# Layer-norm statistics stored in one transfer and read with a stride, and the second and third batch prepared in another order, in a gated cross-attention and expert kernel

## The chip, the cores and the metric

The kernel runs on one core of a Trainium2 chip. The metric is the device time of one launch in microseconds (us), lower is better. One core has TensorE (PE, matrix products), VectorE (DVE), ScalarE (ACT), GpSimd (POOL) and SyncE (SP), which here issues nearly all plain transfers. Each engine works through its own instructions in the order in which they are written, and waits on semaphores for the others.

## What is computed

```python
x = x + jnp.tanh(g_xattn[0]) * _L0_xattn_ref(ctx_1024, _layernorm(x, axis=-1), ...)
x = x + jnp.tanh(g_ffn[0]) * _L0_ffn_ref(_layernorm(x, axis=-1), ...)

def _L0_xattn_ref(x, latents, ...):            # x: the context, latents: the normalised x
    xn, ln = _layernorm(x, gamma_media, beta_media), _layernorm(latents, gamma_lat, beta_lat)
    q = ln @ Wq + bq
    kv = jnp.concatenate([xn, ln], axis=1) @ Wkv + bkv
    k, v = jnp.split(kv, 2, axis=-1)           # 8 heads of 128
    attn = jax.nn.softmax(einsum('bhid,bhjd->bhij', q * DH ** -0.5, k))
    return (attn @ v) @ Wo + bo
```

There are 16 batches of 256 rows of x and 256 rows of context, 256 wide. The attention has 8 heads of 128 over 512 keys (256 of the context, 256 of the latents). The second half, `_L0_ffn_ref`, sends each of the 4096 rows to 2 of 8 experts (256 to 1024 to 256). Everything is float32; each product is made of three products of a high and a low part.

## The kernel before

**Attention by steps.** A step `i` (0 to 127) is one head `h = i % 8` of one batch `b = i // 8`. In step `i` TensorE makes, in this order: the scores of step `i`; the transposes of the probabilities of step `i-1` (`turn`); the units `k` and `q` of step `i+1`, one unit `v`, and the unit `o` of step `i-1` (weights times values); and the output projection of step `i-2`. The units take turns in a ring of three PSUM banks, so the unit `o` of a step starts when the `k` unit of that step has been read. ACT rounds each unit to its high part (`kt_hi`, `qt_hi`, ...), DVE subtracts it for the low part (`kt_lo`, `qt_lo`, ...). DVE also takes the maxima of the scores (`smax`, then `nbias`), ACT the exponentials, and POOL multiplies by the reciprocal sums (`probs`).

**The operand of a batch.** All keys, values and queries of a batch are products with one operand, `kvt`: the normalised rows of x and context, transposed. For batch 0 it is made on the spot. For each later batch `c` it is made ahead, from transposed copies of x and context that the host supplies:

- `load(c)` brings the plain rows (`x_raw`, `c_raw`); `load_turned(c)` brings the transposed ones into `zin` (named `z_turned` in the trace). SP issues both.
- DVE takes mean and variance of the plain rows (`prepare_a(c, 0)` for x, `prepare_a(c, 1)` for the context; BATCH_NORM rows in the trace). POOL turns them into a negated mean and a factor for each row, in `norms` (`prepare(c)`).
- `spread_norms(c)` on SP writes `norms` to DRAM and reads it back to all 128 partitions, as the tile `spread`, so that each column of `zin` finds its mean and its factor.
- DVE adds the mean (`centre(c, k)`) and multiplies by the factor (`normalise_turned(c, k)`), for k = 0 and 1. ACT applies gamma and beta (`scale_turned(c)`, L1047), and POOL splits the result into the high and low part of `kvt` (`split_kv(c)`, L912 and L914).

For batch 1 the calls stand in steps 3 to 5: `centre` and `normalise_turned` in 3 and 4, `scale_turned` at the end of step 4, `split_kv` in step 5 after `probs`. The first unit that needs the `kvt` of batch 1 is the `v` unit of step 5. For batches 2 and later they stand at steps h = 6, 7, 0, 1 and 3. DVE's `prepare_a(2, 0)` stands at the end of step 2.

**Weights.** Each weight is loaded raw, ACT makes the high part (`hi_weights`), DVE or POOL the low part (`lo_weights`). The pieces are `q0`, `k0` (heads 0 and 1), `v0`, `k1`, `q1` (the other six heads), `v1`, `o0`, `o1`. The raw pieces `k1`, `q1`, `o0`, `o1` lie where `spread` lies later, so SP waits for `k1` to be split before it fills `spread`.

**SP's own order.** SP is one queue of issues. Its waits hold up what is written behind them, as here, where the rows of batch 2 stand behind two waits of `spread_norms(1)`:

```python
            load_turned(1)
            spread_norms(1)
            sp.wait_ge(s_routing, N_ROUTING)
            ...
            load(2)
            load_turned(2)
            spread_norms(2)
```

After the attention, the expert part runs over 40 tiles of rows. The change does not touch it.

Of the kernel before, what the change touches and what calls it, by code (L numbers as in the profile page):

```python
# [190 lines left out]
def build(nc, A):  # L191
# [10 lines left out]
    with ExitStack() as top:  # L202
# [45 lines left out]
        with ExitStack() as third:  # L248
# [33 lines left out]
            spread=nc.dram_tensor("mean_and_factor", (B, 2, KEYS), F32, kind="Internal").ap(),  # L282
# [56 lines left out]
def layer(nc, programs, A, sem, alloc, space, early, step, work, lists, ident, iota8, lane, dram,  # L339
# [6 lines left out]
    with ExitStack() as ctx:  # L346
# [141 lines left out]
        s_win = {name: sem(name + "_in") for name in ("k0", "k1", "q0", "q1", "v0", "v1", "o0", "o1")}  # L488
# [166 lines left out]
        def columns(name, at, width, by):  # L655
# [8 lines left out]
                  columns("q1", FIRST_W, rest, "dve"), columns("v1", HALF, HALF, "pool")]  # L664
        for c in range(2):
            heads = slice(c * H // 2, (c + 1) * H // 2)
            pieces.append(("o" + str(c), A["L0_xattn_Wo"][c * INNER // 2:(c + 1) * INNER // 2, :]
                           .rearrange("(h p) n -> p h n", p=P), raw["o" + str(c)], [w[:, heads, :] for w in wo], "dve"))
# [22 lines left out]
        def _(sp):  # L691
# [16 lines left out]
            def load_turned(c):  # L708
# [5 lines left out]
                for name, cols in (("x_turned", slice(T, KEYS)), ("ctx_turned", slice(0, T))):  # L714
                    sp.dma_start(zin[:, :, cols], A[name][c].rearrange("(k p) t -> p k t", p=P)).then_inc(s_turned_in, 16)

            def spread_norms(c):
# [13 lines left out]
                sp.dma_start(spread[:, :, :].rearrange("p r t -> p (r t)"),  # L731
                             dram["spread"][c].rearrange("r t -> (r t)").partition_broadcast(P)).then_inc(s_spread, 16)
# [4 lines left out]
            load_weights("o0", "o1")  # L737
# [8 lines left out]
            load_turned(1)  # L746
            spread_norms(1)
# [4 lines left out]
            load(2)  # L752
# [70 lines left out]
        def _(pool):  # L823
# [22 lines left out]
            def prepare(c):  # L846
# [5 lines left out]
                if c >= 2:  # L852
                    pool.wait_ge(s_norms_out, 64 * (c - 1))
# [102 lines left out]
            for i in range(STEPS + 2):  # L956
# [7 lines left out]
                if i == 5:  # L964
# [44 lines left out]
        def _(act):  # L1009
# [30 lines left out]
            def scale_turned(c):  # L1040
# [3 lines left out]
                for k in range(KD):  # L1044
                    for s in range(2):
                        cols = slice(s * T, (s + 1) * T)
                        last = act.activation(zt[:, k, cols], zin[:, k, cols], ACT.Identity,  # L1047
# [78 lines left out]
            for i in range(STEPS + 2):  # L1126
# [23 lines left out]
                if i == 4:  # L1150
# [52 lines left out]
        def _(pe):  # L1203
            def unit(kind, at):
# [4 lines left out]
                if kind in "kq":  # L1209
                    b, h = at // H, at % H  # L1210
                    if at in (0, FIRST_HEADS):
                        weights_split(pe, kind + str(int(at > 0)))
                    if (kind, at) == ("q", 0):
# [68 lines left out]
            def out_proj(n):  # L1282

                b, h = n // H, n % H
                if n == 0:
                    weights_split(pe, "o0")
                    weights_split(pe, "o1")
# [164 lines left out]
        def _(dve):  # L1452
# [365 lines left out]
            def centre(c, k):  # L1818
# [3 lines left out]
                own.mark(dve.tensor_tensor(zin[:, k, :], zin[:, k, :], spread[:, 0, :], ALU.add))  # L1822

            def normalise_turned(c, k):
                own.wait()
                dve.tensor_tensor(zin[:, k, :], zin[:, k, :], spread[:, 1, :], ALU.mult).then_inc(s_zin, 1)

            for i in range(STEPS + 2):
# [12 lines left out]
                for u in steps[i]:  # L1841
# [16 lines left out]
                if i in (3, 4):  # L1858
                    normalise_turned(1, i - 3)
# [7 lines left out]
                if i == 1:  # L1867
                    lo_weights(dve, "dve", "o0", "o1")
# [101 lines left out]
```

## Time and profile before

| | before |
|---|---|
| median of 3 runs | 1546.45 us (1545.08 to 1552.04) |
| the profiled execution | 1541.18 us, of which the span is 1539.5 us |
| TensorE busy | 1491.3 us, 97% of the span |
| DVE, ACT, POOL busy | 1140.1, 954.1, 568.9 us |
| granted TensorE clock over the span | 0.994 of full speed |

The profiled execution is 5.3 us shorter than the median of the runs. The span runs from its first to its last instruction. All rows are of that execution, with times counted from the span's start.

### The profile page before, as it was taken

The page shows a single profiled execution, that of the slowest core. Times are in us where ns is not written, and L with a number is a line of the kernel's source. Part 1 is how long each engine was busy: PE and PEld are TensorE (multiplying, and loading weights), DVE is VectorE, ACT ScalarE, POOL GpSimd, SP SyncE. Part 2 cuts the span into 40 slices and gives each one's busy share as a digit, 9 for nine tenths or more (in the row PEclk, how much of TensorE's full clock was granted, in tenths as well). Part 3 has the DMA queues.
Part 4 walks back from the last instruction along what each step waited for, and adds up shares of the span by engine and source line. Part 5 has one row for each costly group of instructions (what it writes and reads, how often), then busy time and mean ns, then how long its engine had stood idle before and what let it go on. Part 6 is the DMA issues. An engine that isn't in the chain of part 4 may idle for free. (4 is left out here: it accounts for less than half of the span.)

```text
span 1539.5 us, 29848 instructions
## 1 busy us (share of the span) xinstructions
PE 1491.3 (97%) x10326; PEld 1371.1 (89%) x10326; DVE 1140.1 (74%) x2749; ACT 954.1 (62%) x2057; POOL 568.9 (37%) x654
## 2 busy tenths in 40 slices
PE   8699999999999999999999999999889999999996
PEld 6588898888888888888888989888889999999996
DVE  7567877778777787777778778787686666666685
ACT  6455556556555655655555565655787777777775
POOL 4213334233243333334233342332455454444442
PEclk9999999999999999999999999999999999999999
DMA  5101101011010111101011010012854455545463
GB/s 163 46 14 49 42 22 36 22 49 42 22 35 22 37 36 33 42 21 36 22 49 42 22 36 22 8 57 63 222 122 132 128 146 142 128 128 152 133 175 81
DMA packets 84465, 106.92 MB, mean 69 GB/s; under 512 B 25658, under 2 KB 69495, under 8 KB 84191
## 3 DMA queue, kind: packets, MB, share of 16 engines
q1 hardware_dynamic: 68350, 85.98, 18.1%
q0 software_dynamic: 15824, 18.98, 6.9%
q8 instruction: 87, 1.43, 0.5%
q14 instruction: 60, 0.48, 0.2%
q10 hardware_dynamic: 144, 0.05, 0.0%
HBM read 86.64 MB, written 18.35 MB: 68 GB/s over the span
## 5 line engine op out<-in xcount | busy, mean ns | idle before, releaser
L921 POOL TENSOR_SCALAR probs<-probs,rsum 128x512 f32<-128x512 f32 x256 | 175.1, 695 | 609.9 <-DVE rsum L1598 603.1
L1131 ACT ACTIVATE pt_hi<-turn 128x512 fp32r<-128x512 f32 x256 | 139.5, 597 | 235.1 <-PE turn L1278 233.6
L946 POOL DMA_INDIRECT out_rows<-yo,token x71 | 119.7, 1686 | 206.0 <-DMA out_rows<-yo,token 136.4
L1715 DVE TENSOR_TENSOR ht_lo<-hs,ht_hi 128x512 fp32r<-128x512 f32 x142 | 98.2, 692 | 119.6 <-ACT ht_hi L1098 117.9
L1030 ACT ACTIVATE probs<-score,nbias 128x512 f32<-128x512 f32 x256 | 173.6, 688 | 7.1 <-DVE nbias L1594 7.1
L1592 DVE TENSOR_REDUCE smax<-score 128x1 f32<-128x512 f32 x256 | 168.1, 683 | 7.0 <-PE score L188 6.8
L1089 ACT ACTIVATE hs<-ph,vecs 128x256 f32<-128x256 f32 (+1 forms) x284 | 114.8, 460 | 93.9 <-PE ph L188 86.2
L1835 DVE TENSOR_TENSOR pt_lo<-turn,pt_hi 128x512 fp32r<-128x512 f32 x256 | 164.3, 683 | 9.4 <-ACT pt_hi L1131 8.8
L186 PE MATMUL py<-w_hi,ht_lo 128*128 (+1 forms) x568 | 162.7, 286 | 4.2 <-DVE ht_lo L1715 2.6
L188 PE MATMUL py<-w_hi,ht_hi 128*128 (+1 forms) x568 | 160.6, 283 | 0.0
L187 PE MATMUL py<-w_lo,ht_hi 128*128 (+1 forms) x568 | 160.5, 283 | 0.0
L186 PE MATMUL ring<-pt_hi,v_lo 128*128 128x256 f32 x512 | 147.4, 288 | 13.3 <-DVE kt_lo L1495 11.6
L1018 ACT ACTIVATE kt_hi<-ring,vecs 128x512 fp32r<-128x512 f32 x128 | 88.5, 692 | 93.6 <-PE ring L188 91.4
L188 PE MATMUL ring<-pt_hi,v_hi 128*128 128x256 f32 x512 | 145.9, 285 | 0.0
L186 PE MATMUL ph<-xt_hi,w1s_lo 128*128 128x256 f32 x496 | 141.1, 285 | 4.5 <-DVE xt_lo L1693 4.4
L187 PE MATMUL ring<-pt_lo,v_hi 128*128 128x256 f32 x512 | 145.4, 284 | 0.0
L188 PE MATMUL ph<-xt_hi,w1s_hi 128*128 128x256 f32 x496 | 138.6, 279 | 0.0
L187 PE MATMUL ph<-xt_lo,w1s_hi 128*128 128x256 f32 x496 | 138.4, 279 | 0.0
L1278 PEld LDWEIGHTS turn<-ident,probs 128*128 128x128 f32 x1024 | 120.5, 141 | 17.2 <-POOL probs L921 0.3
L1278 PE MATMUL turn<-ident,probs 128*128 128x128 f32 x1024 | 133.6, 274 | 0.0
L1495 DVE SCALAR_TENSOR_TENSOR kt_lo<-ring,vecs,kt_hi 128x512 fp32r<-128x512 f32 x128 | 95.8, 749 | 49.6 <-ACT kt_hi L1018 42.1
L1022 ACT ACTIVATE ot_hi<-ring,vecs 128x256 fp32r<-128x256 f32 x128 | 61.0, 477 | 100.7 <-PE ring L188 100.0
(243 smaller groups left out, 4685.4 us busy)
## 6 DMA issues: line engine op xcount, KB each, us to landing
w_raw<-in_L_ffn_W SPq DMA_DIRECT2D x45, 1024.0 KB, 18.7
spread<-mean_and_factor SPq DMA_DIRECT2D x15, 512.0 KB, 4.1
xhat_rows<-rows SPq DMA_DIRECT2D x16, 264.0 KB, 2.2
x_raw<-in_x SPq DMA_DIRECT2D x16, 256.0 KB, 3.0
c_raw<-in_ctx SPq DMA_DIRECT2D x16, 256.0 KB, 3.3
out_rows<-x SPq DMA_DIRECT2D x16, 256.0 KB
z_turned<-in_x_turned SPq DMA_DIRECT2D x15, 256.0 KB, 3.8
z_turned<-in_ctx_turned SPq DMA_DIRECT2D x15, 256.0 KB, 4.2
```

What stands on the lines that cost most here:

```text
L186: pe.matmul(out, ll, rh, start=start, stop=False, **kw)
L187: pe.matmul(out, lh, rl, start=False, stop=False, **kw)
L188: return pe.matmul(out, lh, rh, start=False, stop=stop, **kw)
L921: last = pool.tensor_scalar(probs[n % 2][:, t, :], probs[n % 2][:, t, :], rsum[:, n % 2, t:t + 1], 1.0, ALU.mult, ALU.mult)
L946: pool.indirect_dma_start(out=A["out"], out_offset=bass.IndirectOffsetOnAxis(ap=token[:, u:u + 1].bitcast(U32), axis=0), in_=yo_of(t)[:, s ...
L1030: act.activation(probs[n % 2][:, t, :], score[t][:, :], ACT.Exp, scale=SCALE, bias=nbias[:, n % 2, t:t + 1], accum_out=ssum[:, n % 2, t:t ...
L1089: last = act.activation(by_step(hs[n % N_HS], t)[:, g, :], by_step(ph[n % N_PH] if t < WIDE else turned_of(n), t)[:, g, :], ACT.Silu, bias ...
L1131: act.activation(pt[0][:, 2 * t:2 * t + 2, :], turn[t][:, :].rearrange("p (j i) -> p j i", j=2), ACT.Copy).then_inc(s_pthi, 1)
L1278: last = pe.transpose(turn[t][:, j * T + q * P:j * T + (q + 1) * P], probs[n % 2][:, q, (2 * t + j) * P:(2 * t + j + 1) * P], ident[:, :])
L1592: own.mark(dve.tensor_reduce(smax[:, n % 2, t:t + 1], score[t][:, :], AX_X, ALU.max))
L1715: dve.tensor_tensor(lo[:, :], hs[n % N_HS][:, :], hi[:, :].bitcast(F32), ALU.subtract).then_inc(s_hlo, 1)
L1835: dve.tensor_tensor(pt[1][:, 2 * t:2 * t + 2, :], turn[t][:, :].rearrange("p (j i) -> p j i", j=2), pt[0][:, 2 * t:2 * t + 2, :].bitcast(F ...
```

## The change

`norms` leaves in one transfer instead of four. It lies in DRAM as it lies in the tile, so that each partition writes 8 adjacent values, 32 bytes. Before, each of the 4 transfers put 256 single values of 4 bytes into their place. The copy back still moves 4 KB to each partition, but the values of one kind are now 8 elements apart. DVE therefore reads `spread` with a stride of 32 bytes in `centre` and `normalise_turned`. The columns of `zin` change their halves (x first), and ACT reads them accordingly.

The rows of batch 2 are loaded before `spread_norms(1)`. `centre` and `normalise_turned` of batch 1 move from steps 3 and 4 to 2 and 3, `scale_turned(1)` from 4 to 3, `split_kv(1)` from 5 to 4. The six last heads of Wq become two pieces, `q1` (heads 2 and 3) and `q2` (heads 4 to 7). The low part of `q2` is made at the end of step 2, and that of `o1` at the end of step 4.

```diff
-            spread=nc.dram_tensor("mean_and_factor", (B, 2, KEYS), F32, kind="Internal").ap(),
+            spread=nc.dram_tensor("mean_and_factor", (B, P, 2, JT), F32, kind="Internal").ap(),
...
-                       q1=alloc(raws, "q1_raw", [P, KD, INNER - FIRST_W]),
+                       q1=alloc(raws, "q1_raw", [P, KD, FIRST_W]),
+                       q2=alloc(raws, "q2_raw", [P, KD, INNER - 2 * FIRST_W]),
...
-        spread = sb("spread", [P, 2, KEYS])
+        spread = sb("spread", [P, P, 2, JT])
...
-                for tiles, cols in ((slice(0, TT), slice(T, KEYS)), (slice(TT, JT), slice(0, T))):
-                    with nc.allow_non_contiguous_dma(reason="a value of each row"):
-                        for r in range(2):
-                            sp.dma_start(dram["spread"][c, r, cols].rearrange("(j p) -> p j", p=P), norms[:, r, tiles])\
-                                .then_inc(s_norms_out, 16)
-                sp.wait_ge(s_norms_out, 64 * c)
+                sp.dma_start(dram["spread"][c], norms[:, :, :]).then_inc(s_norms_out, 16)
+                sp.wait_ge(s_norms_out, 16 * c)
...
-            load_weights("o0", "o1")
+            load_weights("o0", "q2", "o1")
...
             load_turned(1)
+            load(2)
             spread_norms(1)
...
-            load(2)
             load_turned(2)
...
-                if i == 5:
+                if i == 4:
                     split_kv(1)
...
-                if i == 4:
+                if i == 3:
                     scale_turned(1)
...
                 if i == 1:
-                    hi_weights(act, "o0", "o1")
+                    hi_weights(act, "o0", "q2")
                 if i == 2:
+                    hi_weights(act, "o1")
...
                 own.wait()
-                dve.tensor_tensor(zin[:, k, :], zin[:, k, :], spread[:, 1, :], ALU.mult).then_inc(s_zin, 1)
+                by_rows = zin[:, k, :].rearrange("p (j i) -> p j i", j=JT)
+                dve.tensor_tensor(by_rows, by_rows, spread[:, :, 1, :].rearrange("p i j -> p j i"), ALU.mult).then_inc(s_zin, 1)
...
-                        if i in (3, 4):
-                            centre(1, i - 3)
+                        if i in (2, 3):
+                            centre(1, i - 2)
...
-                if i in (3, 4):
-                    normalise_turned(1, i - 3)
+                if i in (2, 3):
+                    normalise_turned(1, i - 2)
...
                 if i == 1:
-                    lo_weights(dve, "dve", "o0", "o1")
+                    lo_weights(dve, "dve", "o0")
+                if i == 2:
+                    lo_weights(dve, "dve", "q2")
+                if i == 4:
+                    lo_weights(dve, "dve", "o1")
```

The program of DVE, before, from the low part of Wo at the end of step 1 to the middle of step 3 (`smax` opens a step, a name in brackets is the semaphore waited for, `x2` is two such rows in turn):

```order
L681 TENSOR_TENSOR wo_lo<-o_raw,wo_hi 128x1024 [waits weights_hi] x2
L1592 TENSOR_REDUCE smax<-score 128x1 [waits scores] x2
...
L1495 SCALAR_TENSOR_TENSOR kt_lo<-ring,vecs,kt_hi 128x512 [waits unit_hi]
L1495 SCALAR_TENSOR_TENSOR qt_lo<-ring,vecs,qt_hi 128x256 [waits unit_hi]
L1598 RECIPROCAL rsum<-ssum 128x2 [waits exp]
L1492 TENSOR_TENSOR v_lo<-ring,v_hi 128x512 [waits unit_hi]
L1495 SCALAR_TENSOR_TENSOR ot_lo<-ring,vecs,ot_hi 128x256 [waits unit_hi]
L1459 BN_STATS stats_a<-x_raw 128x6 [waits z_ready,x_in2]
L1459 BN_STATS stats_a<-x_raw 128x6
```

The same stretch of DVE's program in the changed kernel:

```order
L684 TENSOR_TENSOR wo_lo<-o_raw,wo_hi 128x1024 [waits weights_hi]
L1595 TENSOR_REDUCE smax<-score 128x1 [waits scores] x2
...
L1498 SCALAR_TENSOR_TENSOR kt_lo<-ring,vecs,kt_hi 128x512 [waits unit_hi]
L1826 TENSOR_TENSOR z_turned<-z_turned,spread 128x512 [waits spread_in,turned_in]
L1498 SCALAR_TENSOR_TENSOR qt_lo<-ring,vecs,qt_hi 128x256 [waits unit_hi]
L1601 RECIPROCAL rsum<-ssum 128x2 [waits exp]
L1831 TENSOR_TENSOR z_turned<-z_turned,spread 128x512 [waits dve_self]
L1495 TENSOR_TENSOR v_lo<-ring,v_hi 128x512 [waits unit_hi]
L1498 SCALAR_TENSOR_TENSOR ot_lo<-ring,vecs,ot_hi 128x256 [waits unit_hi]
L684 TENSOR_TENSOR wq_lo<-q_raw,wq_hi 128x2x512 [waits weights_hi]
L1462 BN_STATS stats_a<-x_raw 128x6 [waits z_ready,x_in2]
```

One of the two low parts of Wo has left the end of step 1. Step 2 has taken in an add and a multiply with `spread`, and the low part of `q2`, ahead of the statistics of batch 2.

The issues of SP, before, from the transposed rows of batch 1 to those of batch 2:

```order
L715 DMA z_turned<-in_ctx_turned 128x2x256
L724 DMA mean_and_factor<-norms 128x2x1 [waits z_ready,rs_a]
L724 DMA mean_and_factor<-norms 128x2x1 x3
L731 DMA spread<-mean_and_factor 128x1024 [waits weights_lo_pool,norms_out]
L751 DMA expert_lists<-pad_ids 128x128 [waits routing_consts]
...
L696 DMA x_raw<-in_x 128x2x256
L700 DMA c_raw<-in_ctx 128x2x256 [waits z_ready]
L715 DMA z_turned<-in_x_turned 128x2x256 [waits zt_ready]
```

The same stretch of SP's issues in the changed kernel:

```order
L718 DMA z_turned<-in_ctx_turned 128x2x256
L699 DMA x_raw<-in_x 128x2x256
L703 DMA c_raw<-in_ctx 128x2x256 [waits z_ready]
L724 DMA mean_and_factor<-norms 128x8 [waits z_ready,rs_a]
L730 DMA spread<-mean_and_factor 128x1024 [waits weights_lo_pool,norms_out]
L751 DMA expert_lists<-pad_ids 128x128 [waits routing_consts]
...
L718 DMA z_turned<-in_x_turned 128x2x256 [waits zt_ready]
```

The plain rows of batch 2 now stand ahead of the waits for `norms`, and four transfers of `norms` have become one.

The program of POOL, before, from the statistics of batch 2 (in step 3) to step 6; each pair of `probs` is one step:

```order
L856 TENSOR_SCALAR norms<-mv_a 128x4
L921 TENSOR_SCALAR probs<-probs,rsum 128x512 [waits rsum]
L921 TENSOR_SCALAR probs<-probs,rsum 128x512
L921 TENSOR_SCALAR probs<-probs,rsum 128x512 [waits rsum]
L921 TENSOR_SCALAR probs<-probs,rsum 128x512
L912 CAST kvt_hi<-zt 128x1024 [waits zt_ready]
L914 TENSOR_TENSOR kvt_lo<-zt,kvt_hi 128x1024 [waits pool_self]
```

The same stretch of POOL's program in the changed kernel:

```order
L855 TENSOR_SCALAR norms<-mv_a 128x4
L920 TENSOR_SCALAR probs<-probs,rsum 128x512 [waits rsum]
L920 TENSOR_SCALAR probs<-probs,rsum 128x512
L911 CAST kvt_hi<-zt 128x1024 [waits zt_ready]
L913 TENSOR_TENSOR kvt_lo<-zt,kvt_hi 128x1024 [waits pool_self]
L920 TENSOR_SCALAR probs<-probs,rsum 128x512 [waits rsum]
L920 TENSOR_SCALAR probs<-probs,rsum 128x512
```

The split of `kvt` for batch 1 now stands behind the `probs` of step 4 instead of those of step 5.

## Rows read from the trace of the kernel before

**Rows 1.** The page: busy us and share of each engine.

```profile
PE 1491.3 (97%) x10326; PEld 1371.1 (89%) x10326; DVE 1140.1 (74%) x2749; ACT 954.1 (62%) x2057; POOL 568.9 (37%) x654
```

**Rows 2.** Windows, steps 1 to 5: us, PE, PEld, DVE, ACT, POOL busy, PE clock.

```profile
22.96:32.83 9.87, 7.67 (x45) 6.33 (x44) 8.52 (x19) 5.64 (x11) 7.01 (x13) 1.00 0.05 1
32.83:42.42 9.59, 8.16 (x53) 7.01 (x51) 7.25 (x13) 6.87 (x14) 1.84 (x3) 1.00 0.03 1
42.42:56.16 13.74, 9.67 (x52) 8.51 (x51) 7.37 (x18) 4.62 (x11) 1.72 (x2) 0.88 0.29 89
56.16:64.05 7.89, 7.89 (x52) 7.08 (x51) 6.67 (x16) 4.50 (x11) 2.57 (x5) 1.00 0.00 0
64.05:81.33 17.28, 9.96 (x52) 8.64 (x51) 5.36 (x12) 6.49 (x14) 5.45 (x6) 0.80 0.32 62
```

**Rows 3.** TensorE's waits: total us, times, longest; first 0 to 100 us.

```profile
PE ring L186 <- POOL kvt_lo L914: 7.3, 1, 7.3
PE ring L186 <- DVE kt_lo L1495: 6.7, 3, 4.1
...
PE ring L186 <- DVE kt_lo L1495: 3.5, 12, 0.3
```

**Rows 4.** Timeline of DVE: start, duration, instruction, idle before it and its releaser.

```profile
24.40 1.75 DVE L681 TENSOR_TENSOR wq_lo<-q_raw,wq_hi 128x1536 fp32r<-128x1536 f32 x1
34.49 2.36 DVE L681 TENSOR_TENSOR wo_lo<-o_raw,wo_hi 128x1024 fp32r<-128x1024 f32 x2 [0.47 <-ACT wo_hi L674]
36.77 1.28 DVE L1592 TENSOR_REDUCE smax<-score 128x1 f32<-128x512 f32 x2
39.36 0.74 DVE L1495 SCALAR_TENSOR_TENSOR kt_lo<-ring,vecs,kt_hi 128x512 fp32r<-128x512 f32 x1
48.09 0.75 DVE L1459 BATCH_NORM_STATS2 stats_a<-x_raw 128x6 f32<-128x256 f32 x2 [5.19 <-DMA x_raw<-in_x]
```

**Rows 5.** Timeline of SP's issues.

```profile
30.41 1.91 SPq L724 DMA_DIRECT2D mean_and_factor<-norms  x4
41.75 0.33 SPq L731 DMA_DIRECT2D spread<-mean_and_factor  x1
43.51 0.41 SPq L696 DMA_DIRECT2D x_raw<-in_x  x1
```

**Rows 6.** DMA issues, 0 to 100 us: KB each, us from issue to landing.

```profile
spread<-mean_and_factor SPq DMA_DIRECT2D x2, 512.0 KB, 4.4
bg<-in_L_ffn_bg SPq DMA_DIRECT2D x1, 4.0 KB, 4.7
vecs<-in_vectors ACTq DMA_DIRECT2D x1, 48.0 KB, 2.2
```

**Rows 7.** Timeline of POOL, steps 0 to 5, and one later batch.

```profile
24.79 3.60 POOL L681 TENSOR_TENSOR wkv_lo<-v_raw,wkv_hi 128x1024 fp32r<-128x1024 f32 x1 [1.85 <-ACT wkv_hi L674]
63.09 1.74 POOL L921 TENSOR_SCALAR probs<-probs,rsum 128x512 f32<-128x512 f32 x2 [3.94 <-DVE rsum L1598]
70.98 1.36 POOL L921 TENSOR_SCALAR probs<-probs,rsum 128x512 f32<-128x512 f32 x2 [6.16 <-DVE rsum L1598]
72.29 1.04 POOL L912 CAST kvt_hi<-zt 128x1024 fp32r<-128x1024 f32 x1
...
461.89 2.41 POOL L914 TENSOR_TENSOR kvt_lo<-zt,kvt_hi 128x1024 fp32r<-128x1024 f32 x1
```

**Rows 8.** Timeline of TensorE (step 5) and ACT (end of step 4).

```profile
75.89 0.77 PE L186 MATMUL ring<-wkv_hi,kvt_lo 128*128 128x512 f32 x1 [7.32 <-POOL kvt_lo L914]
...
63.91 2.07 ACT L1047 ACTIVATE zt<-z_turned,vecs 128x256 f32<-128x256 f32 x4
```

**Rows 9.** Instructions on `z_turned`, all batches: ns min/median/max; first and last start.

```profile
L1822 DVE TENSOR_TENSOR z_turned<-z_turned,spread x30: 678/681/684, 52.3 to 955.6; 128x512 f32<-128x512 f32 x30
```

**Rows 10.** Timeline of DVE in a later batch, around one add of `centre`.

```profile
480.85 0.48 DVE L1495 SCALAR_TENSOR_TENSOR qt_lo<-ring,vecs,qt_hi 128x256 fp32r<-128x256 f32 x1 [0.36 <-ACT qt_hi L1020]
...
482.48 0.48 DVE L1495 SCALAR_TENSOR_TENSOR ot_lo<-ring,vecs,ot_hi 128x256 fp32r<-128x256 f32 x1 [0.46 <-ACT ot_hi L1022]
```

More of the change, by code:

```diff
@@ L487, in layer @@
         s_vec, s_small = sem("vectors_in"), sem("small_in")
-        s_win = {name: sem(name + "_in") for name in ("k0", "k1", "q0", "q1", "v0", "v1", "o0", "o1")}
+        s_win = {name: sem(name + "_in") for name in ("k0", "k1", "q0", "q1", "q2", "v0", "v1", "o0", "o1")}
         s_x = [sem(f"x_in{i}") for i in range(3)]
@@ L663, in layer @@
                   columns("v0", 0, HALF, "dve"), columns("k1", FIRST_W, rest, "pool"),
-                  columns("q1", FIRST_W, rest, "dve"), columns("v1", HALF, HALF, "pool")]
+                  columns("q1", FIRST_W, FIRST_W, "dve"), columns("v1", HALF, HALF, "pool")]
         for c in range(2):
+            if c:
+                pieces.append(columns("q2", 2 * FIRST_W, rest - FIRST_W, "dve"))
             heads = slice(c * H // 2, (c + 1) * H // 2)
@@ L713, in load_turned @@
                     sp.wait_ge(s_zt, c - 1)
-                for name, cols in (("x_turned", slice(T, KEYS)), ("ctx_turned", slice(0, T))):
+                for name, cols in (("x_turned", slice(0, T)), ("ctx_turned", slice(T, KEYS))):
                     sp.dma_start(zin[:, :, cols], A[name][c].rearrange("(k p) t -> p k t", p=P)).then_inc(s_turned_in, 16)
@@ L730, in spread_norms @@
                     sp.wait_ge(s_zin, KD * (c - 1))
-                sp.dma_start(spread[:, :, :].rearrange("p r t -> p (r t)"),
-                             dram["spread"][c].rearrange("r t -> (r t)").partition_broadcast(P)).then_inc(s_spread, 16)
+                sp.dma_start(spread[:, :, :, :].rearrange("p i r j -> p (i r j)"),
+                             dram["spread"][c].rearrange("i r j -> (i r j)").partition_broadcast(P)).then_inc(s_spread, 16)
             load(0)
@@ L852, in prepare @@
                 if c >= 2:
-                    pool.wait_ge(s_norms_out, 64 * (c - 1))
+                    pool.wait_ge(s_norms_out, 16 * (c - 1))
                 own.wait()
@@ L1046, in scale_turned @@
                         cols = slice(s * T, (s + 1) * T)
-                        last = act.activation(zt[:, k, cols], zin[:, k, cols], ACT.Identity,
+                        last = act.activation(zt[:, k, cols], zin[:, k, (1 - s) * T:(2 - s) * T], ACT.Identity,
                                               scale=gamma[:, s, k:k + 1], bias=beta[:, s, k:k + 1])
@@ L1212, in unit @@
                         weights_split(pe, kind + str(int(at > 0)))
+                    if (kind, at) == ("q", 2 * FIRST_HEADS):
+                        weights_split(pe, "q2")
                     if (kind, at) == ("q", 0):
@@ L1286, in out_proj @@
                     weights_split(pe, "o0")
+                if n == H // 2:
                     weights_split(pe, "o1")
@@ L1821, in centre @@
                 dve.wait_ge(s_spread, 16 * c)
-                own.mark(dve.tensor_tensor(zin[:, k, :], zin[:, k, :], spread[:, 0, :], ALU.add))
+                by_rows = zin[:, k, :].rearrange("p (j i) -> p j i", j=JT)
+                own.mark(dve.tensor_tensor(by_rows, by_rows, spread[:, :, 0, :].rearrange("p i j -> p j i"), ALU.add))
             def normalise_turned(c, k):
                 own.wait()
-                dve.tensor_tensor(zin[:, k, :], zin[:, k, :], spread[:, 1, :], ALU.mult).then_inc(s_zin, 1)
+                by_rows = zin[:, k, :].rearrange("p (j i) -> p j i", j=JT)
+                dve.tensor_tensor(by_rows, by_rows, spread[:, :, 1, :].rearrange("p i j -> p j i"), ALU.mult).then_inc(s_zin, 1)
             for i in range(STEPS + 2):
```

## Prediction

> **What bounds the kernel now.** I read the page first: TensorE is busy 97% of the span [rows 1]. So a gain can only come from stretches in which it stands still. Its waits from 100 to 900 us add up to 3.5 us, while two causes in the first 100 us hold 7.3 and 6.7 us [rows 3]. The windows place them. An undisturbed step takes 7.9 us (step 4: 7.89). Steps 1, 2, 3 and 5 take 9.87, 9.59, 13.74 and 17.28 us [rows 2]. In the two long ones the mean granted clock is 0.88 and 0.80 instead of 1.00: TensorE had stood idle and went on for a while at the lower of its two levels (1.2 instead of 2.4 GHz). The excess over 7.9 us is 1.7 us in step 2, 5.8 in step 3 and 9.4 in step 5; of the last, 7.3 are the wait and 2.1 the slow clock behind it.
>
> The timeline says what ends each wait. In step 3 DVE sat idle 5.19 us for the plain rows of batch 2 before it could take the maxima [rows 4]. SP issued these rows at 43.51, because it had stood behind the store of `norms`, issued at 30.41, whose landing released the next issue at 41.75 [rows 5]. In steps 1 and 2 DVE was late with low parts of weights: `wq_lo` took 1.75 us, the two `wo_lo` 2.36 us, and `smax` of step 2 followed without a gap at 36.77 [rows 4]. In step 5 TensorE came to its `v` unit at 75.89 - 7.32 = 68.57, which is 4.5 us into the step [rows 8], and waited for POOL, which began the split only behind the `probs` of that step, at 72.29 [rows 7].
>
> **The change, part by part.** I follow it along the path; for steps 1 to 3 that is DVE.
>
> Step 1. `q1` shrinks from 1536 to 512 elements of a partition. A two-input instruction of 512 elements takes 0.68 us [rows 9], so DVE saves 1.75 - 0.68 = **1.1 us** ahead of step 1's maxima, and step 2 begins at 31.8 instead of 32.8.
>
> Step 2. One `wo_lo` (half of 2.36, 1.2 us) goes from its front. DVE comes to `smax` at 36.77 - 1.1 - 1.1 = 34.6, still behind the scores. So the step gains another **1.1 us**, and `kt_lo` of step 2 ends at 39.36 + 0.74 - 2.2 = 37.9. Step 3 begins on TensorE at 40.2.
>
> Now `centre(1, 0)` asks for `spread`, and DVE would stall there if it were late. POOL's low part of `v1` took 3.60 us beside DVE's `wq_lo` [rows 7]; with the short `q1` the statistics and `norms` are ready some 0.8 us sooner, so SP issues the store at 29.6. Its landing is unseen in this form. The nearest rows: a 48 KB load landed after 2.2 us, and `bg`, also 128 pieces of 32 bytes, after 4.7 us with other loads in flight [rows 6]; the present store of single values held SP from 32.3 to 41.75, 9.4 us [rows 5]. The bounds are 2.2 and 9.4. I take 3.5, between the first two, since a quarter of the pieces leaves in a quarter of the issues while the queue is nearly idle. The read back lands 4.4 us after its issue [rows 6]. 29.6 + 3.5 + 4.4 gives 37.5, against 37.9: no wait, but with 0.4 us to spare.
>
> Step 3. The 5.19 us of waiting go, since the rows are now asked for ahead of the store of `norms`, so before 30 us, and land some 14 us ahead of their use (before, they came within 5 us of the issue at 43.51). In their place DVE takes in 0.68 + 0.68 us for the add and the multiply [rows 9] and 1.2 us for `q2` (1024 elements, as one `wo_lo`). After `ot_lo` of step 2 (waiting for TensorE and ACT, it ends near 40.7) come `q2` to 41.9 and the statistics to 42.8; `smax`, `nbias`, `pt_lo` and `kt_lo` then end near 46.0. TensorE, from 40.2, is through its scores, `turn`, `k`, `q` and `v` 5.8 us later, also at 46.0. So it just does not wait: no idle time, no slow clock, and the step costs 7.9: **5.8 us** gained, with no slack under it. Every us that DVE needs more in step 2 is lost again.
>
> Step 4 keeps its 7.9 us and begins at 48.2. ACT applies gamma and beta (2.07 us [rows 8]) by 50.7, just as `turn` of step 4 is ready. The low part of `o1` adds 1.2 us of DVE at its end; DVE idles over 1 us in such a step (6.67 busy of 7.89 [rows 2]).
>
> Step 5 begins at 56.1. The `probs` of step 4 start 63.09 - 56.16 = 6.9 us into it [rows 7], at 55.1. They took 1.74 us beside the adds of batch 1, which are now gone from this step, and take 1.36 as in step 5: to 56.4. The cast (1.04) and `kvt_lo` (2.41) follow [rows 7], with 0.1 us between them: to 60.0. TensorE needs it at 56.1 + 4.5 = 60.6. `kvt_lo` now runs beside DVE's `o1`; beside `wq_lo` a POOL instruction of the same 1024 elements took 3.60 us instead of 2.41 [rows 7], 1.2 us more, of which some 0.6 us is slack. I put down 0.4 us for the wait that may be left here and the thin margins above, and gain 9.4 - 0.4 = **9.0 us**.
>
> Everything behind it. `scale_turned` and its wait keep their order, SP's issues of later batches only come sooner, and the three issues saved for each batch and the 9 us of store are hidden: DVE never waits there for `spread`. Those parts cost and bring nothing. If the cover went, the store would hold up the rows of the batch after next, which have whole steps to arrive.
>
> The stride. 60 instructions (30 adds, 30 multiplies) now read one operand at every eighth value. No row shows such a read over a long operand. Below it is nothing: one element in about 1 ns is what the contiguous ones take (512 in 0.68 us). Above I take twice the time for each element, 0.53 us more. In a later batch DVE waits 0.36 us for `qt_hi` and 0.46 us for `ot_hi` behind the add [rows 10], so 0.8 us are absorbed in each step, and 0.53 stays hidden 56 times. It counts in steps 2 and 3 alone, where nothing is slack: up to 4 x 0.53 = 2.1 us, of which the second pair is partly covered by the return to TensorE's pace; 1.6 us. I take the lower end for the sum, since no row shows a cost, and keep the other as a rival.
>
> The Trainium skill speaks against it: "Advanced Engine Details and Errata", Memory Cachelines, says that SBUF has 16-byte lines, and that an access pattern which goes to another line with each element pays a penalty; the page gives no figure. Here every element of `spread` would be on a line of its own. No run of this case shows it yet; by that rule the sum would be lower by the rival's 1.6 us or more.
>
> **Sum.** 1.1 + 1.1 + 5.8 + 9.0 = 17.0 us. The profiled execution goes from 1541.2 to 1524.2 us. The median of the runs is 5.3 us above that execution, so I forecast 1546.45 - 17.0 = **1529.5 us**, 1.1% faster.
>
> **Rivals.**
> - *The stride costs double.* For it: an unseen access form, in the two steps without slack. Against: the operand that is read and written stays contiguous. Gain 17.0 - 1.6 = 15.4, with some 0.4 more through a later split: 1531.5 us.
> - *The store of `norms` stays slow.* If its time is that of a landing in DRAM and not of the 1024 single pieces, SP goes on at 29.6 + 9.4 = 39.0 and `spread` lands at 43.4. DVE waits 5.5 us in step 2, TensorE's clock drops as in step 3 of before (1.7 us), and the gain is about 10: 1536.5 us. Against it: the DMA engines were nearly idle in that time, yet 256 pieces in each of four transfers are what differs from all fast rows.
> - *The split stays late.* POOL's `kvt_lo` takes 3.60 us beside `o1`, and `probs` of step 4 come a little late. TensorE waits 2 to 3 us in step 5: 1532 us.
> - *The change does not do what it says.* The load comes sooner, but DVE's taken-in work and another wait fill both holes, and less than 8 us is left: 1540 us or more.
> - *Slower.* The strided read is so slow that DVE becomes the bound in every batch. 0.8 us of each are absorbed; over the four steps of a batch a further backlog of about 2.5 us can be carried. At 3.0 us for an instruction (2.3 more) the four of a batch exceed that by 3.5 us, and 14 batches lose 49 us against 17 gained: 1578 us. It turns at about 2.1 us for an instruction, three times that of now. Against it: no row of DVE is that slow for 512 elements.
>
> **How the numbers follow.** Chances: forecast 0.50, stride 0.25, slow store 0.08, late split 0.07, not as said 0.07, slower 0.03. The runs of before spread over 7 us, and the measurement tells about 0.5% (7.7 us) from no change. The first four cases, 0.90, are beyond it: faster 0.90, same 0.07, slower 0.03. The range reaches from 1523 (all gained, nothing left in step 5, a few us of spread) to 1537 (slow store); it leaves out the last two cases and the tails.
>
> **What will show it.** The windows from one step's first score product to the next: steps 1 to 5 of about 8.8, 8.4, 7.9, 7.9 and 8.0 us, at full granted clock. DVE has no wait for `x_raw` in step 2. SP's issue of `spread` follows the store by 3 to 5 us, not by 9. `z_turned<-z_turned,spread` stays at 0.68 us, or stands near 1.2 if the rival holds. The wait for `kvt_lo` is under 1 us. I am wrong if a wait over 2 us stands at DVE's add in step 2 (`spread` late), if steps of later batches grow past 7.95 us (the stride reaches TensorE), or if the total moves while steps 1 to 5 do not.

## The result, and the profile after

The changed kernel takes 1528.8 us (median of four runs, 1526.99 to 1531.17) against 1547.96 us before (four runs, 1545.08 to 1552.04). The ratio is 0.9875, with a 95% interval of 0.9847 to 0.9903: 15.0 to 23.7 us faster. The forecast was 1529.5 us.

The page of the changed kernel, the span and the engines' busy time, answers to [rows 1]:

```profile
span 1527.2 us, 29807 instructions
...
PE 1490.1 (98%) x10326; PEld 1369.5 (90%) x10326; DVE 1164.1 (76%) x2750; ACT 951.6 (62%) x2058; POOL 576.1 (38%) x654
```

TensorE does the same work in a shorter span. DVE has grown by 24 us, nearly all of it hidden beside TensorE's work, as the windows will show. These are steps 1 to 5 and then step 18 of the changed kernel, in the columns of [rows 2]:

```profile
24.19:32.99 8.80, 7.65 (x46) 6.33 (x45) 7.45 (x19) 5.63 (x11) 6.00 (x14) 1.00 0.02 4
32.99:41.43 8.44, 8.16 (x52) 7.00 (x51) 7.23 (x12) 6.74 (x14) 1.18 (x2) 1.00 0.25 80
41.43:50.45 9.02, 8.38 (x53) 6.94 (x52) 8.95 (x18) 5.55 (x12) 2.18 (x3) 1.00 0.01 2
50.45:58.53 8.08, 8.08 (x53) 7.00 (x52) 6.58 (x17) 6.40 (x14) 4.03 (x8) 1.00 0.34 107
58.53:67.43 8.90, 8.39 (x53) 7.05 (x52) 7.79 (x12) 4.60 (x10) 6.01 (x5) 1.00 0.07 23
164.57:176.35 11.78, 9.55 (x52) 8.39 (x51) 7.47 (x17) 6.37 (x14) 4.03 (x8) 0.86 0.52 112
```

The five steps took 58.37 us and take 43.24. Both long steps are gone, and with them the low clock. Step 3 is now a step in which DVE is full (8.95 busy of 9.02). TensorE's waits in the first 100 us answer to [rows 3]:

```profile
PE ring L186 <- DVE kt_lo L1498: 2.2, 4, 1.1
PE ring L186 <- POOL kvt_lo L913: 0.4, 1, 0.4
```

Of 7.3 and 6.7 us, 0.4 and 2.2 are left. SP's issues answer to [rows 5] (first the plain rows of batch 2):

```profile
16.72 0.68 SPq L699 DMA_DIRECT2D x_raw<-in_x  x1
...
30.60 0.34 SPq L724 DMA_DIRECT2D mean_and_factor<-norms  x1
32.02 0.34 SPq L730 DMA_DIRECT2D spread<-mean_and_factor  x1
```

The read back follows its store by 1.4 us; before it was 11.3 us (30.41 to 41.75). And the instructions on `z_turned`, which answer to [rows 9] (ns min/median/max, then first and last start):

```profile
L1826 DVE TENSOR_TENSOR z_turned<-z_turned,spread x30: 1120/1154/1228, 39.0 to 945.0; 128x512 f32<-128x512 f32 x30
L1831 DVE TENSOR_TENSOR z_turned<-z_turned,spread x30: 1098/1171/1174, 40.6 to 952.9; 128x512 f32<-128x512 f32 x30
```

The strided read costs 0.48 us for each instruction, 1.7 times the 681 ns of before. The steps of later batches don't show it. Laid side by side, none of the 117 steps from 6 to 123 other than 18 differs by more than 0.03 us between the two profiles (steps 66, 68 and 70 take 8.47, 8.78 and 8.30 us in both), and their sums agree within 0.01.

**The account of the profiled pair.** The two spans differ by 12.3 us: steps 1 to 5 give 15.1; step 18 takes 3.3 back (8.48 to 11.78, the last window above); step 0 starts 1.3 us later (14.87 to 16.13); from step 124 to the end 1.7 us are gained; the rest is equal. The medians differ by 19.2 us. The last section shows that the expert part varies between executions of one and the same program by more than this gap, so what the change does is best read in the windows of steps 1 to 5, which in the changed kernel repeat within 0.03 us.

### The profile page after: what moved, and what is told of

It reads as the page before. It is cut to its first block, busy times and chain, and to the rows that moved or that the text cites. A ratio compares the mean times of both kernels' runs of the same rounds, so it can differ in the third digit from the quotient of the medians.

```text
span 1527.2 us, 29807 instructions
## 1 busy us (share of the span) xinstructions
PE 1490.1 (98%) x10326; PEld 1369.5 (90%) x10326; DVE 1164.1 (76%) x2750; ACT 951.6 (62%) x2058; POOL 576.1 (38%) x654
## 4 chain that ended last, share of the span: by engine, by line
PE 83%; DVE 10%; ACT 2%; DMA 2%; issue 1%; POOL 1%; another core or an unknown queue 0%; DVEq 0%; ACTq 0%; POOLq 0%
PE ring L186 12%; PE ring L188 12%; PE ring L187 12%; PE turn L1280 6%; PE py L186 4%; PE py L188 4%; PE py L187 4%; PE ph L186 4%; PE ph L188 4%; PE ph L187 4%; PE score L186 3%; PE score L188 3%; PE score L187 3%; PE proj L187 2%; PE proj L186 2%; PE proj L188 2%
```

## The experiments

Windows of steps 1 to 5 are given as a list with their sum. Ratios are to the kernel before, run beside each on the same chip.

### The two kernels once more

No edit, one execution each.

> The kernel before, unchanged, for a second profile. The profiled execution of before lies 5 us under its own runs, and the changed kernel's does not lie under its runs. If that is a matter of single executions, the windows of steps 1 to 5 come out as in the first profile (9.9, 9.6, 13.7, 7.9, 17.3 us) and the rest of the span differs. If the early stalls themselves vary (the store of the statistics lands at another time), step 3 or 5 is several us longer here.

> The changed kernel, unchanged, for a second profile. Steps 1 to 5 again 8.8, 8.4, 9.0, 8.1 and 8.9 us within 0.1. If the 3.3 us hole in step 18 and the 1.3 us before step 0 belong to the change, they stand here again; if they are chance of one execution, step 18 takes 8.5 us and step 0 begins near 14.9 us.

Before: 9.87, 9.57, 13.69, 8.77, 17.75, together 59.65 us, in an execution of 1559.94 us. Changed: 8.80, 8.44, 9.02, 8.10, 8.87, together 43.23, in one of 1536.91 us. The changed kernel's windows repeat to 0.03 us, while its execution is 8 us longer than the one profiled first; before moved by 1.3 us in the windows (steps 4 and 5) and by 18.8 in all. This second pair differs by 23.0 us: 16.4 of them stand in steps 1 to 5, 8.4 behind step 124 and 4.2 in a hole of before in step 106; the changed kernel gives 5.3 back in step 18 (13.73) and 0.7 ahead of step 0.

### Only the early load, and only the store in one transfer

The first moves one call in the kernel before. The second puts the new layout of `norms` and the strided reads into the kernel before, and leaves all calls where they were.

```diff
             load_turned(1)
+            load(2)
             spread_norms(1)
...
-            load(2)
             load_turned(2)
```

```diff
-                for tiles, cols in ((slice(0, TT), slice(T, KEYS)), (slice(TT, JT), slice(0, T))):
...
+                sp.dma_start(dram["spread"][c], norms[:, :, :]).then_inc(s_norms_out, 16)
+                sp.wait_ge(s_norms_out, 16 * c)
```

> The kernel before with one edit: the plain rows of batch 2 are loaded ahead of the store of the statistics. My theory: step 3 falls from 13.7 to 7.9 us, steps 1, 2 and 5 stay at 9.9, 9.6 and 17.3, so 5.8 us are gained. Rival: the add in step 3 then waits for the statistics (they land near 46, DVE wants them near 47), and step 3 stays above 9 us.

> The kernel before with the statistics stored in one transfer and read with the stride, the order of everything else as before. SP comes to the plain rows of batch 2 some 8 us sooner (near 34 us instead of 43.5), which is ahead of DVE's need at 43, so my theory is that this edit alone also empties the hole of step 3: 5.8 us less 0.5 to 1 for the strided reads, step 3 at 8 to 9 us; step 5 stays at 17.3. So the early load and the store would not add up. Rival: the rows come late all the same and only part of the hole goes (step 3 at 10 us or more).

Steps 3 and 5, first of the kernel with only the early load, then of the one with only the new store:

```profile
42.36:50.26 7.90, 7.90 (x52) 7.09 (x51) 6.88 (x16) 4.49 (x11) 0.97 (x1) 1.00 0.33 89
...
58.16:75.53 17.37, 10.05 (x52) 8.77 (x51) 5.35 (x12) 6.47 (x14) 5.44 (x6) 0.80 0.22 62
```

```profile
42.72:50.62 7.90, 7.90 (x53) 7.08 (x51) 7.24 (x16) 4.49 (x11) 0.96 (x1) 1.00 0.01 2
...
58.52:75.64 17.12, 9.81 (x52) 8.45 (x51) 5.74 (x12) 6.56 (x14) 5.91 (x6) 0.80 0.19 62
```

Each empties the hole of step 3 alone, and each leaves step 5 as it was. The sums are 52.61 and 52.36 us, 5.8 and 6.0 less than before; the ratios are 0.9956 [0.9936, 0.9976] and 0.9942 [0.9912, 0.9971]. For step 3 the two edits do the same thing twice, since a short store lets SP reach the rows soon enough. SP's issues in the kernel with only the new store:

```profile
30.71 0.34 SPq L721 DMA_DIRECT2D mean_and_factor<-norms  x1
...
33.88 0.42 SPq L696 DMA_DIRECT2D x_raw<-in_x  x1
```

The rows leave at 33.88 instead of 43.51. The strided instructions stand here in steps 3 and 4, where DVE has slack, and cost nothing.

### The old store in the changed kernel

The four transfers and the plain layout come back; loads, calls and weights stay as changed.

```diff
-                sp.dma_start(dram["spread"][c], norms[:, :, :]).then_inc(s_norms_out, 16)
...
+                        for r in range(2):
+                            sp.dma_start(dram["spread"][c, r, cols].rearrange("(j p) -> p j", p=P), norms[:, r, tiles])\
+                                .then_inc(s_norms_out, 16)
```

> The changed kernel with the old store and the old layout: four transfers of single values, adjacent reads; batch 1 still prepared a step sooner and the rows of batch 2 still loaded ahead. My theory: the statistics land 8 us later, near 44.5 us, where DVE wants them at 39.0, so DVE waits 5 us in step 2 for spread, the adds take 0.68 us again, TensorE's clock falls once, and steps 1 to 5 together take 4 to 6 us more than in the changed kernel (43.2). Rival: the store's time is hidden here too, steps 1 to 5 take 41 to 43 us, and the one transfer earned nothing.

Steps 2 and 3, DVE's wait for `spread`, and SP's issues of this kernel, three views:

```profile
32.86:47.75 14.89, 8.36 (x53) 6.97 (x51) 6.07 (x12) 7.74 (x15) 0.48 (x1) 0.90 0.21 46
47.75:57.55 9.80, 9.80 (x51) 8.58 (x51) 9.36 (x20) 4.52 (x11) 2.73 (x3) 0.81 0.01 2
```

```profile
46.61 0.69 DVE L1829 TENSOR_TENSOR z_turned<-z_turned,spread 128x512 f32<-128x512 f32 x1 [7.61 <-DMA spread<-mean_and_factor]
```

```profile
30.46 1.90 SPq L727 DMA_DIRECT2D mean_and_factor<-norms  x4
...
41.31 0.33 SPq L734 DMA_DIRECT2D spread<-mean_and_factor  x1
```

DVE stood 7.6 us in step 2, where the forecast's rival of a slow store had put 5.5, and TensorE went on at a clock of 0.81. The sum is 50.31 us, 7.1 more than with the new store; the ratio is 0.9926 [0.9884, 0.9967]. The interval of the ratio overlaps that of the changed kernel (0.9847 to 0.9903), so this reading rests on the windows and the wait. The new store is what makes the earlier `centre` affordable. It belongs to the move of batch 1, more than to the hole of step 3.

### The reads side by side, and other strides

Both kernels change only what DVE reads from `spread`, and so leave out the mean and the factor of each row.

```diff
-                own.mark(dve.tensor_tensor(by_rows, by_rows, spread[:, :, 0, :].rearrange("p i j -> p j i"), ALU.add))
+                own.mark(dve.tensor_tensor(zin[:, k, :], zin[:, k, :], flat[:, 0:KEYS], ALU.add))
...
-                dve.tensor_tensor(by_rows, by_rows, spread[:, :, 1, :].rearrange("p i j -> p j i"), ALU.mult).then_inc(s_zin, 1)
+                dve.tensor_tensor(zin[:, k, :], zin[:, k, :], flat[:, KEYS:2 * KEYS], ALU.mult).then_inc(s_zin, 1)
```

The second kernel reads every second value (add, k = 0), four runs of 128 adjacent values (multiply, k = 0), every fourth (add, k = 1) and every sixteenth (multiply, k = 1):

```diff
+                                               flat.rearrange("p (i s) -> p s i", s=2)[:, 0, :], ALU.add))
...
+                                      flat.rearrange("p (j i) -> p j i", j=4)[:, :, 0:P], ALU.mult).then_inc(s_zin, 1)
...
+                                               flat.rearrange("p (i s) -> p s i", s=4)[:, 0:2, :], ALU.add))
...
+                                      flat.rearrange("p (i s) -> p s i", s=16)[:, 0:8, :], ALU.mult).then_inc(s_zin, 1)
```

> The changed kernel, but DVE adds and multiplies with 512 adjacent values of spread each (columns 0 to 511 and 512 to 1023), so not with the mean and factor of each row. It shows what the stride costs: the instructions fall from 1.15 to 0.68 us. My theory: four of them stand in steps 2 and 3 with no slack, so step 3 falls from 9.0 to 8.0 or less and the whole by 1 to 2 us; steps of later batches do not change. Rival: step 3's extra us comes from the low part of q2 and the statistics alone, and step 3 stays above 8.7.

> The changed kernel, with four ways to read the second operand of 512 values (not the mean and factor of each row): every 2nd value (8 bytes apart), every 4th in two runs (16 bytes), four runs of 128 adjacent values, and every 16th in eight runs (64 bytes). If what counts is whether neighbours share a line of 16 bytes, every 2nd value and the adjacent runs take 0.68 us, every 4th and every 16th 1.15 as every 8th does. Rival: the cost grows with the distance (64 bytes dearer than 32), or comes from the many runs rather than from the distance (then the adjacent runs are dear as well).

The tiles of the two kernels (ns min/median/max), first the adjacent reads; then steps 3 and 4 of that kernel; then every second value, every fourth, the four runs, every sixteenth:

```profile
L1826 DVE TENSOR_TENSOR z_turned<-z_turned,spread x30: 678/681/684, 38.9 to 947.6; 128x512 f32<-128x512 f32 x30
```

```profile
41.31:49.42 8.11, 8.11 (x52) 7.00 (x51) 8.00 (x18) 5.47 (x13) 1.71 (x3) 1.00 0.01 2
49.42:57.32 7.90, 7.90 (x52) 7.08 (x51) 5.85 (x15) 6.38 (x14) 3.17 (x7) 1.00 0.41 121
```

```profile
L1827 DVE TENSOR_TENSOR z_turned<-z_turned,spread x15: 678/681/686, 39.1 to 931.5; 128x512 f32<-128x512 f32 x15
L1830 DVE TENSOR_TENSOR z_turned<-z_turned,spread x15: 1067/1089/1093, 47.2 to 947.7; 128x512 f32<-128x512 f32 x15
L1838 DVE TENSOR_TENSOR z_turned<-z_turned,spread x15: 669/681/683, 40.1 to 939.8; 128x512 f32<-128x512 f32 x15
L1842 DVE TENSOR_TENSOR z_turned<-z_turned,spread x15: 1045/1056/1072, 48.6 to 955.6; 128x512 f32<-128x512 f32 x15
```

With adjacent reads steps 3 and 4 fall from 9.02 and 8.08 to 8.11 and 7.90: of steps 1 to 5 the stride costs TensorE 1.1 us in these two (42.18 us for the five; ratio 0.9835 [0.9797, 0.9873]). It is not the number of runs that costs (four runs: 681 ns), nor a step of 8 bytes (681 ns). From 16 bytes on the instruction takes 0.4 to 0.5 us more, and a step of 64 bytes costs no more than one of 16. The Trainium skill says that SBUF has lines of 16 bytes, and that two accesses must fall on a line to hide what its fetch costs ("Advanced Engine Details and Errata", Memory Cachelines). The rows agree: two values on a line are free, one on each line is not. They give the size, which the page does not. Steps 1 to 5 of this second kernel took 42.28 us: 8.80, 8.45, 8.11, 8.02 and 8.90. That places the cost. Its pair for k = 0, in step 2, takes the short 0.68 us each and its pair for k = 1, in step 3, the long 1.06 to 1.09, and yet step 3 falls to 8.11. So 0.9 of the 1.1 us come from the pair in step 2, just ahead of the step without slack, and some 0.1 from the pair in step 3.

### The split in step 5 again

```diff
-                if i == 4:
+                if i == 5:
                     split_kv(1)
```

> The changed kernel with the split of batch 1's operand back behind the probs of step 5. My theory: the 7.3 us wait and the slow clock return, step 5 takes 17 us instead of 8.9, and nothing before it changes. Rival: the earlier add and scaling had brought it forward by themselves, and step 5 stays under 12 us.

Step 5 and TensorE's wait in it:

```profile
58.76:76.98 18.22, 10.89 (x53) 9.58 (x52) 6.53 (x12) 4.55 (x10) 5.09 (x5) 0.72 0.04 13
```

```profile
70.60 0.77 PE L186 MATMUL ring<-wkv_hi,kvt_lo 128*128 128x512 f32 x1 [7.33 <-POOL kvt_lo L913]
```

The wait of before is back to 0.01 us (7.32 and 7.33), though all the rest of the change is in place. The place of the split behind one pair of `probs` more decides step 5, 9.3 us of it.

### The low part of `o1` one step later

```diff
-                if i == 4:
+                if i == 5:
                     lo_weights(dve, "dve", "o1")
-                if i == 5:
                     constants()
```

> The changed kernel with the low part of o1 on DVE at the end of step 5 instead of step 4. In the changed kernel that instruction (2.1 us instead of 1.2) ran beside POOL's split (3.2 us instead of 2.4). My theory: each slows the other; apart, they take 1.2 and 2.4 us, the 0.4 us wait for the split goes, and step 5 falls from 8.9 to 7.9 or 8.2 us. Rival: the split is slowed by DVE's other reads anyway (3 us or more) and step 5 stays above 8.6.

POOL and DVE, first in the changed kernel, then with `o1` later; step 5 of the latter ends the block:

```profile
58.88 1.04 POOL L911 CAST kvt_hi<-zt 128x1024 fp32r<-128x1024 f32 x1
58.92 2.08 DVE L684 TENSOR_TENSOR wo_lo<-o_raw,wo_hi 128x1024 fp32r<-128x1024 f32 x1
60.01 3.24 POOL L913 TENSOR_TENSOR kvt_lo<-zt,kvt_hi 128x1024 fp32r<-128x1024 f32 x1
62.23 1.04 DVE L1597 TENSOR_SCALAR nbias<-smax 128x2 f32<-128x2 f32 x1
```

```profile
59.87 2.39 POOL L913 TENSOR_TENSOR kvt_lo<-zt,kvt_hi 128x1024 fp32r<-128x1024 f32 x1
60.71 1.57 DVE L1597 TENSOR_SCALAR nbias<-smax 128x2 f32<-128x2 f32 x1
66.84 1.21 DVE L684 TENSOR_TENSOR wo_lo<-o_raw,wo_hi 128x1024 fp32r<-128x1024 f32 x1
```

```profile
58.39:66.45 8.06, 8.06 (x53) 7.01 (x52) 6.48 (x11) 4.45 (x10) 4.92 (x5) 1.00 0.12 39
```

Beside each other the two instructions take 3.24 and 2.08 us, apart 2.39 and 1.21. The starts and ends suggest a chain: `wo_lo` begins just behind POOL's cast `kvt_hi` and ends 1.08 us after it (61.00 and 59.92), `kvt_lo` begins inside `wo_lo` and ends 2.25 us after it, and `nbias` begins inside `kvt_lo` and ends with it (63.27 and 63.25). Apart, step 5 takes 8.06 us instead of 8.90, and the wait for `kvt_lo` is gone. But `nbias` isn't freed: it takes 1.57 us here and again ends with `kvt_lo` (62.28 and 62.26). What the move gains is that `kvt_lo` ends 3.87 us into step 5 instead of 4.72. The sum is 42.48 us (one execution, 1533.23 us).

### The low part of `q2` on POOL, alone and with the former

```diff
-                pieces.append(columns("q2", 2 * FIRST_W, rest - FIRST_W, "dve"))
+                pieces.append(columns("q2", 2 * FIRST_W, rest - FIRST_W, "pool"))
...
+                if i == 1:
+                    lo_weights(pool, "pool", "q2")
...
-                if i == 2:
-                    lo_weights(dve, "dve", "q2")
```

> The changed kernel with the low part of q2 on POOL (step 1, behind its probs, at 33.5 us) instead of on DVE in step 2. It takes 1.4 us off DVE where my prediction found no slack. Theory: step 3 falls from 9.0 to 7.9 us, step 2 stays at 8.4 or a few tenths more for the shared reads. Rival: TensorE then waits for the stride's share only, or POOL's work slows DVE's maxima and low parts in step 2 by as much as it takes off, and steps 2 and 3 together stay above 17.2 us (17.46 in the changed kernel).

> The changed kernel with both edits: the low part of o1 in step 5, that of q2 on POOL. If they add up, steps 1 to 5 take 41.3 us instead of 43.2, and the whole is 2 us (0.13%) below the changed kernel, about 1.3% below before, which no timing of some rounds can tell from the changed kernel's own ratio (0.9875); the windows can. Rival: what step 2 gains, step 3 or 4 gives back, and the sum stays above 42.5.

Steps 2 and 3 with `q2` on POOL, and what meets in step 2:

```profile
32.53:41.87 9.34, 8.16 (x53) 7.01 (x51) 8.13 (x12) 6.86 (x14) 3.66 (x3) 1.00 0.23 72
41.87:49.97 8.10, 8.10 (x53) 7.01 (x51) 7.98 (x18) 5.43 (x12) 2.42 (x3) 1.00 0.01 2
```

```profile
35.18 2.50 POOL L684 TENSOR_TENSOR wq_lo<-q_raw,wq_hi 128x1024 fp32r<-128x1024 f32 x1 [2.19 <-ACT wq_hi L677]
36.65 1.06 DVE L1599 TENSOR_SCALAR nbias<-smax 128x2 f32<-128x2 f32 x1
```

Step 3 gained 0.9 us of the 1.1 that my theory gave it, and step 2 lost the same: `nbias`, an instruction of 0.17 us, was held until POOL's `wq_lo` was done (37.71 and 37.68). The sum is 43.06, no gain. With `o1` later as well it is 42.16 us (8.79, 9.35, 8.08, 7.89, 8.05), where 41.3 was expected, and the ratio is 0.9908 [0.9883, 0.9933]. Its interval overlaps that of the changed kernel, so the 1.1 us of the windows can't be told in the time.

### Eight instructions more in ACT's program

To the last kernel, which kept the hole of step 18:

```diff
+                if i in (9, 10):
+                    for n in range(4):
+                        act.activation(warm[:, 4 * (i - 9) + n:4 * (i - 9) + n + 1], iota8[:, n:n + 1], ACT.Copy)
```

> The changed kernel with the low part of o1 in step 5 and that of q2 on POOL, and with 8 one-element copies of no use added to ACT's program in steps 9 and 10. In all seven profiles so far whose program starts from the changed kernel, step 18 takes 3 to 7 us too long: ACT starts nothing for 3.5 to 6.7 us while the loads of a batch are in flight, and no engine is named as the releaser; in none of the four that start from the kernel before does this stand in step 18. Theory: ACT's program is brought in by pieces, and here the fetch of the next piece falls behind those loads; 8 instructions more move the border by half a step, so step 18 falls to 8.5 to 9 us (a hole may turn up elsewhere). Rival: the hole hangs on the transfers of that step and not on the place in ACT's program; then it stays in step 18 with 3 us or more. Steps 1 to 5 as before this edit, 42.2 us.

Step 18 took 12.38 us, with ACT idle 4.90 us ahead of `pt_hi`, the same instruction as before the shift (5.62 us there); the ratio is 0.9907 [0.9886, 0.9929]. (By then nine profiles showed the hole, not seven; with this one they are ten.) A hole bound to a place in ACT's program would have moved by eight instructions. It stayed, which speaks against that theory. Even without a shift the hole isn't tied to one instruction: in the second execution of the changed kernel it stands ahead of `kt_hi` and not between the two `pt_hi`.

## Why the prediction was right, step by step

The path was right in each of the five steps, and so was the time, 0.7 us off; one cost was wrongly put at nothing, one landing too long, and part of the closeness is luck. The terms of the sum, forecast and measured in the profiled pair:

| step | forecast | measured |
|---|---|---|
| 1 | 1.1 | 1.07 |
| 2 | 1.1 | 1.15 |
| 3 | 5.8 | 4.72 |
| 4 | 0 | -0.19 |
| 5 | 9.0 | 8.38 |
| sum | 17.0 | 15.13 |

- **Steps 1 and 2**: the smaller `q1` and the `wo_lo` that left gave what their rows said.
- **Step 3**: the wait for `x_raw` went, and the clock stayed at its upper level. "With no slack under it" held too, and that is where the term was mis-sized. The stride had been put down at nothing. It was 0.48 us for each instruction, close to the 0.53 of the rival, and with it gone steps 3 and 4 give back 1.1 us. The rest, 0.2 us in step 3, stays open: `q2` took 1.40 us and not the 1.2 that I took from `wo_lo`, but with adjacent reads it took 1.25 and step 3 still 8.11. The rival priced the stride at 1.6 us on the path, so its mechanism was true and its cost lies between the two forecasts.
- **The rows of batch 2** were asked for at 16.7. That this edit alone would earn the term is shown, and so is that the store alone would. The prediction gave the whole 5.8 us to the load and did not see that the two overlap.
- **The store**: I took 3.5 us for its landing; it landed after 1.4 (median of its rows, and the gap to the next issue says the same). The lower bound, 2.2 us, was too high. The slack of 0.4 us under DVE's `centre` was therefore larger, and DVE did not wait. With the old store DVE waits 7.6 us, so the short store was needed.
- **Step 5**: the split's place carries the term. It is 0.6 us short, since step 5 takes 8.90 us where 8.0 was forecast for the windows (8.3 by the sum). `kvt_lo` beside `o1` cost 0.85 us, against 1.2 as the upper bound, and TensorE waited 0.35 us for it, as put down (0.4). Not foreseen was the second victim: `nbias` took 1.04 us instead of 0.17, and `kt_lo` came late. Moving `o1` gives the 0.8 us of the step back, though not `nbias`, which still waits for the end of `kvt_lo` (1.57 us); `kt_lo` starts 5.0 us into the step instead of 5.9.
- **Everything behind it**: steps of later batches stayed the same within 0.03 us, so the 0.5 us of stride in each step of 56 is hidden, as argued. Two things were not foreseen in stretches where I had put down nothing: a hole of 3.3 us in step 18, and a step 0 that starts some 1.3 us later. The last section takes up both. They did not decide the sign.
- **From the sum to the median**: 15.1 us in the windows lies at the lower end of the interval (15.0 to 23.7). The forecast's gain was 17.0; the medians gave 19.2 us, 1.5 of them because the median of before rose with its fourth run, and the profiled executions alone would have given 12.2. The last two kernels of the experiments, with 1.1 us less in the windows, gained only some 14 us (ratios 0.9908 and 0.9907). So that the median came out at the forecast's 1529.5 is partly luck.

## What to carry to other kernels

When two edits remove one wait, test each alone before adding their worth; what the second buys may be that some other call can be moved. After a move, look at the steps that have lost their slack: an instruction that costs nothing anywhere else (a strided operand, a low part made beside an instruction of the other of DVE and POOL) is paid in full there, so it should stand where DVE idles. Small values that are stored for a later broadcast are worth keeping in the order in which they lie on the chip, if the reader's stride stays under 16 bytes or its engine has time to spare.

## What the runs showed of the hardware

**DVE and POOL hold each other up, and the order of starting decides.** The same pair in the profile of before (first block) and in its second execution (second block), just ahead of step 0:

```profile
7.03 0.74 DVE L1773 TENSOR_SCALAR z<-c_raw,mv_a,rs_a 128x256 f32<-128x256 f32 x2 [0.26 <-POOL rs_a L954]
7.56 1.34 POOL L681 TENSOR_TENSOR wq_lo<-q_raw,wq_hi 128x512 fp32r<-128x512 f32 x1 [0.57 <-ACT wq_hi L674]
```

```profile
6.88 1.27 POOL L681 TENSOR_TENSOR wq_lo<-q_raw,wq_hi 128x512 fp32r<-128x512 f32 x1
6.95 1.68 DVE L1773 TENSOR_SCALAR z<-c_raw,mv_a,rs_a 128x256 f32<-128x256 f32 x2 [0.26 <-POOL rs_a L954]
```

The row of `z` is two instructions (`x2`). Where POOL starts before the second of them, they take 0.9 us more, and step 0 starts about 1 us later (15.72 instead of 14.87). ACT's `wq_hi`, which POOL needs, had waited for the first raw piece of Wq, so it hangs on when that piece lands. Of the four profiles that start from the kernel before, one went this way; of the ten that start from the changed kernel, all (1.67 to 1.71 us). So most of the 1.3 us by which step 0 is late goes with the change (it starts at 15.67 to 16.38 in those ten). The piece `q1`, issued behind `q0` and now a third as large, may let `q0` land sooner; no run tested that. The Trainium skill says of DVE's modes that use two ports, which `tensor_scalar` can enter, that the engine which issues first gets the pair of ports that DVE shares with GpSimd for the whole instruction, and the other is fully blocked ("SBUF — State Buffer", Who interferes with whom). These rows agree, and so does `nbias`, another `tensor_scalar`: it ends with POOL's instruction in each case (1.04, 1.06 and 1.57 us instead of 0.17).

**A hole in step 18 that came with the change.** ACT in the changed kernel, step 18:

```profile
166.61 0.60 ACT L1130 ACTIVATE pt_hi<-turn 128x512 fp32r<-128x512 f32 x1
170.68 0.60 ACT L1130 ACTIVATE pt_hi<-turn 128x512 fp32r<-128x512 f32 x1 [3.47 <-remote]
```

ACT starts nothing for 3.5 us while loads of a batch are in flight, and the profile names no engine that it waited for (`remote` is an unknown releaser); TensorE waits, and its clock drops to 0.86. All ten profiles of kernels that start from the changed one show it (step 18 longer by 3.3 to 6.8 us), none of the four that start from the one before. Those have a like hole in step 106 in two cases (12.69 and 11.63 us). Its cause stays open. A shift of ACT's program did not move it. A load of 8 KB of instructions starts 2.4 to 4.9 us into step 18 in all fourteen profiles, with the hole and without, so that load alone isn't the cause. That it hangs on the transfers of that step is a guess which no run tested. Whoever finds it gains some 3 to 7 us.

**The expert part differs between executions of one program.** From step 124 to the end, before took 490.1 us in one execution and 502.0 in the other. TensorE's wait for the gathered rows in that part (total, times, longest), of the first and of the second:

```profile
PE px L1305 <- DMA xg<-xhat_rows,token: 1.9, 2, 1.3
```

```profile
PE px L1305 <- DMA xg<-xhat_rows,token: 9.6, 5, 2.7
```

In the other profiles the stretch took 488 to 501 us. The mean is 494.8 us over the four that start from the kernel before and 493.8 over the ten others, so the change has no clear share in it. A change worth 15 us in the first 70 us can be told in the total only over several runs, and one of 1 us can't.
